# A delta-rule mixer's last turns and an expert dispatch put into one stage, with the order of each engine's queue rewritten

## The reference

```python
h = h + _L0_attn_ref(_layernorm(h))      # gated delta rule, 16 heads of 64
h = h + _L0_ffn_ref(_layernorm(h))       # 32 experts, 4 per token, 256 places each
...
# mixer, per head: S = S * exp(g); S = S + k (beta * (v - S k)); o = S q
# then o * silu(z), RMS norm, W_out
# experts:
probs = softmax(x @ gate_w.T); topk_w, topk_idx = top_k(probs, 4); topk_w /= topk_w.sum(-1)
pos = place of the row among the rows of its expert, in token order
buf = zeros((E, C + 1, h)).at[e_s, slot].set(x[t_s])          # the dispatch
expert_out = silu_and_mul(buf @ w_gate_up) @ w_down
routed = scatter-add of expert_out * topk_w (0 where pos >= 256)
shared = silu_and_mul(x @ shared_w_gate_up) @ shared_w_down
return routed + shared
```

## Time and profile before

| | us |
|---|---|
| median of 3 runs (lowest, highest) | 2871.31 (2869.2, 2872.5) |
| profiled execution, first to last instruction | 2864.9 |
| PE busy in it | 2380.9 (83%) |
| DVE busy | 2012.3 (70%) |
| ACT busy | 1292.8 (45%) |
| POOL busy | 851.1 (30%) |
| mean granted TensorE clock, share of full speed | 0.908 |

### The profile page before, as it was taken

How to read it: one execution, slowest core, us unless ns; L and a number is a source line. 1 busy time by engine, 2 the same in 40 slices (tenths; PEclk the granted TensorE clock), 3 DMA queues, 4 the chain that set the end, 5 groups by cost and what they waited for, 6 DMA issues and landing times. The chain is left out here.

```text
span 2864.9 us, 53688 instructions
## 1 busy us (share of the span) xinstructions
PE 2380.9 (83%) x19286; PEld 1823.1 (64%) x19286; DVE 2012.3 (70%) x4812; ACT 1292.8 (45%) x3118; POOL 851.1 (30%) x708
## 2 busy tenths in 40 slices
PE   7999998996468989898989898777552948899798
PEld 6777777885446777676767677555431845577454
DVE  4888884334468888888888888952663447896673
ACT  1444442111457777676767777743000314444132
POOL 2111100001023333333333333331577037650110
PEclk9999998996679999999999999988665978899799
DMA  4210001003102222222222222221211952210000
GB/s 152 88 59 29 13 7 56 22 25 121 64 20 49 53 52 53 54 53 54 53 54 53 53 53 52 49 68 35 88 37 19 295 174 74 57 47 1 24 22 27
DMA packets 274342, 168.97 MB, mean 59 GB/s; under 512 B 182847, under 2 KB 250318, under 8 KB 273728
## 3 DMA queue, kind: packets, MB, share of 16 engines
q1 hardware_dynamic: 247949, 140.28, 17.3%
q0 software_dynamic: 26112, 25.03, 3.3%
HBM read 99.23 MB, written 73.45 MB: 60 GB/s over the span
## 5 line engine op out<-in xcount | busy, mean ns | idle before, releaser
L1333 POOL TENSOR_TENSOR qd<-decay,qm 114x456 f32<-114x456 f32 x128 | 163.7, 1299 | 551.0 <-DVE qm L1448 467.0
L1838 PEld LDWEIGHTS d_ps<-d_xT,resid 128*128 128x128 f32 x1024 | 197.1, 194 | 46.1 <-issue 29.0
L1838 PE MATMUL d_ps<-d_xT,resid 128*128 128x228 f32 x1024 | 215.7, 363 | 12.3 <-DMA d_xT<-normed_t 12.3
L1429 DVE TENSOR_TENSOR ue<-ue,elim_tmp 128x30 f32<-128x30 f32 (+14 forms) x480 | 211.9, 441 | 16.8
L2578 POOL DMA_INDIRECT s_eo<-rows_y,slots_all x128 | 154.3, 1206 | 146.5 <-POOLq L2390 108.5
L1491 DVE SCALAR_TENSOR_TENSOR y_v<-raw,taps,y_v 128x228 f32<-128x228 f32 x384 | 164.4, 500 | 47.4 <-ACT y_v L1643 47.4
L1427 DVE TENSOR_TENSOR elim_tmp<-ue 128x30 f32<-128x30 f32 (+14 forms) x480 | 179.1, 373 | 25.2 <-issue 9.8
L1605 ACT ACTIVATE decay<-d_ps,gates 114x114 f32<-114x114 f32 x512 | 138.0, 362 | 85.0 <-DVE nt L1461 50.9
L1491 DVE SCALAR_TENSOR_TENSOR y_qk<-raw,taps,y_qk 128x228 f32<-128x228 f32 x384 | 145.0, 452 | 23.6 <-ACT y_qk L1643 23.6
L2142 POOL DMA_INDIRECT rows_x<-r_xn,slot x128 | 144.1, 1126 | 52.4 <-issue 50.6
L1616 ACT ACTIVATE gl<-upto,gates 114x114 f32<-114x114 f32 x512 | 156.1, 393 | 0.4
(11 more groups left out here) (343 smaller groups left out, 5559.7 us busy)
## 6 DMA issues: line engine op xcount, KB each, us to landing
rows_x<-zero_row SPq DMA_DIRECT2D x4, 2048.0 KB
ue<-blocks_n SPq DMA_DIRECT2D x16, 512.0 KB, 5.0
blocks_u<-ue SPq DMA_DIRECT2D x16, 512.0 KB, 2.8
blocks_v<-on SPq DMA_DIRECT2D x16, 512.0 KB, 2.9
e_x<-rows_x SPq DMA_DIRECT2D x32, 256.0 KB, 4.5
e_gu<-L_ffn_w_gate_up SPq DMA_DIRECT2D x32, 256.0 KB, 4.4
rows_y<-e_y SPq DMA_DIRECT2D x32, 256.0 KB, 3.4
blocks_n<-nt SPq DMA_DIRECT2D x96, 64.0 KB
```

Of the source, the lines that this page charges most:

```text
L1333: pool.tensor_tensor(qd[p.par][s][:, hs(u), :].rearrange("p (a o b) t -> p a o b t", o=2, b=2)[:, :, o], e[o][:, :, :].rearrange("p (a b) ...
L1429: step = dve.tensor_tensor(ue[:, 0:j, j + 1:], ue[:, 0:j, j + 1:], part, ALU.subtract)
L1838: last = pe.matmul(ps[:, f % 2, (t % 2) * W:(t % 2 + 1) * W], w_qkv[:, k, t * 128:(t + 1) * 128], xT[:, k, :], start=(k == 0), stop=(k == ...
```

## The change

`route` goes; its work is done in `delta_net`, in turns 15 to 17, which each engine now runs from its own `last_turns` with the order written out by hand. Turn 14 and all before it stay.

- *Rows in slots from 0 on.* `c.resid` is used from slot 0; the output weights move from slots 24 to 31 to 26 to 33. SP loads groups 0 to 3 when the last projection is done, 4 and 5 when the last gate product is, 6 when the output products of pair 13 are, 7 at the very end; for groups 6 and 7 (slots 24 to 31) the first two of eight pieces of the output weights are kept a second time (`w_late`, in `d_xT`'s place).
- *Dispatch from turn 15.* `scatter(0)` begins in the turn that makes the last decay weights; the normalised and turned rows lie in tiles that the mixer no longer uses (`raw`, `y_qk`, `y_v`, `nt`, `qd`, `ue`), the slots in four new ones.
- *Solves in halves.* Pairs 14 and 15 (`Pair.last`) are solved sample after sample, two chains at a time, in banks 0, 1, 6 and 7 (`vbank`, `xbank`); banks 2 to 5 go to the routing.
- *Other engines.* For these pairs DVE scales the gates (pair 14 and 15) and clears the update tiles, which POOL did.
- *Shared expert last.* All `gate_up` and `down` come after the last solve.

The diff, cut to its core. In it each call stands on a line of its own; here several share one. SP:

```diff
+                def load_rows(g):
+                    if g >= GROUPS - 2:
+                        for s in range(2):
+                            sp.wait_ge(h_out[s], 16 * (2 * g + 2))
+                    sp.dma_start(c.resid[:, g * GS:(g + 1) * GS, :],
+                                 hid[g * GS:(g + 1) * GS].rearrange("b s d -> s b d")).then_inc(hid_in[g], 16)
+                def last_turns():
+                    iteration(Pair(0, 14))
+                    sp.wait_ge(qkv_mm, PAIRS * 8)
+                    for g in range(EARLY):
+                        load_rows(g)
+                    sp.dma_start(w_late[:, :, :], dr["L0_attn_W_out_t"].rearrange("(k p) n -> p k n", p=128)[:, 0:2, :]).then_inc(late_in, 16)
+                    iteration(Pair(0, 15), proj=False)
...
+                    sp.wait_ge(wo_mm, 2 * PAIRS - 4)
+                    load_rows(6)
+                    iteration(Pair(0, 16), a=False, proj=False, rows=(4, 5))
+                    iteration(Pair(0, 17), a=False, proj=False, z=False)
+                    sp.wait_ge(wo_mm, 2 * PAIRS)
+                    load_rows(7)
```

POOL, from the end of turn 15's own work on (`done` is pair 14, later pair 15):

```diff
+                def scatter(g, s):
+                    pool.wait_ge(slot_r, g + 1)
+                    for k in range(TOPK):
+                        pool.indirect_dma_start(
+                            out=rows_x, out_offset=bass.IndirectOffsetOnAxis(ap=slot[g % XN][:, s, k:k + 1], axis=0),
+                            in_=rxn_t[g][:, s, :], in_offset=None, bounds_check=SLOTS - 1, oob_is_err=False).then_inc(scat[g % XN], 16)
...
+                    power(1); scatter(0, 0); power(2); scatter(0, 1); scatter(0, 2); scatter(0, 3)
+                    mask_blocks(p); done = Pair(0, 14); scatter(1, 0); scatter(1, 1)
+                    gate_power(done, 0); gate_power(done, 1); power(3); scatter(1, 2); scatter(1, 3)
+                    for s in range(GS):
+                        scatter(2, s)
+                    scatter(3, 0); power(4); scatter(3, 1); power(5); scatter(3, 2); scatter(3, 3)
+                    done = Pair(0, 15); scatter(4, 0); scatter(4, 1); scatter(4, 2); scatter(4, 3); power(6)
+                    scatter(5, 0); gate_power(done, 0); gate_power(done, 1)
+                    scatter(5, 1); scatter(5, 2); scatter(5, 3); scatter(6, 0)
+                    power(7); scatter(6, 1); scatter(6, 2); scatter(6, 3)
+                    for s in range(GS):
+                        scatter(7, s)
```

DVE, from `weights(p, 3)` of turn 15 on (`p` is pair 15, `r` pair 14, then pair 15):

```diff
+                    statistics(0); residual(done, 0); eliminate(r, 24, 29); normalise(0)
+                    weights(p, 4); query_mask(p, 2); weights(p, 5); eliminate(r, 29, 31); turn_inverse(r)
+                    gate_silu(r, 1); query_mask(p, 3); residual(done, 1); weights(p, 6); weights(p, 7)
+                    gate_silu(r, 2); gate_silu(r, 3); statistics(1); choose(0); clear_corner(r, 0); normalise(1)
+                    place(0); statistics(2); choose(1); share(0); gated(r, 0); gated(r, 1); clear_corner(r, 1)
+                    clear_rows(Pair(0, 15), 0); place(1); share(1); normalise(2); gated(r, 2); gated(r, 3); ch.end()
+                    r, done = Pair(0, 15), Pair(0, 14)
+                    gate_mean(done, 0); gate_mean(done, 1); clear_rows(r, 1); eliminate(r, 1, 5); choose(2)
+                    statistics(3); place(2); scale_rows(done, 0); scale_rows(done, 1); gate_silu(r, 0); gate_silu(r, 1)
+                    normalise(3); share(2); residual(done, 0); eliminate(r, 5, 14); gate_silu(r, 2); gate_silu(r, 3)
+                    choose(3); residual(done, 1); eliminate(r, 14, 18); place(3); eliminate(r, 18, 26)
+                    statistics(4); eliminate(r, 26, 31); turn_inverse(r); normalise(4); share(3); statistics(5)
+                    choose(4); place(4); clear_corner(r, 0); normalise(5); share(4); statistics(6); choose(5)
+                    gated(r, 0); gated(r, 1); clear_corner(r, 1); place(5); share(5); gated(r, 2); gated(r, 3)
+                    done = Pair(0, 15)
+                    gate_mean(done, 0); gate_mean(done, 1); normalise(6); scale_rows(done, 0); scale_rows(done, 1)
+                    shared(0); choose(6); residual(done, 0); residual(done, 1); place(6); share(6); shared(1)
+                    add_shared(0); statistics(7); shared(2); add_shared(1); normalise(7); shared(3); add_shared(2)
+                    choose(7); shared(4); add_shared(3); place(7); share(7)
...
```

PE, from the last output product of turn 15 on; pair 15 is solved like pair 14, with groups 4 and 5 between:

```diff
+                    output_product(done, 1); turn(0); gate_logits(0)
+                    value(r, 0, True); value(r, 1, True); join(r, 0, True); join(r, 1, True); counts(0)
+                    inverse(r, 0); inverse(r, 1); turn(1); substitute(r, 0, 0); substitute(r, 0, 1); gate_logits(1)
+                    carry(r, 0); carry(r, 1); substitute(r, 1, 0); substitute(r, 1, 1); counts(1)
+                    outputs(r, 0); outputs(r, 1); join(r, 2, True); join(r, 3, True); value(r, 2, True); value(r, 3, True)
...
+                    turn(4); value(r, 0, False); gate_logits(4); value(r, 1, False); counts(4); join(r, 0, False); join(r, 1, False)
...
+                    done = Pair(0, 15)
+                    gate_up(0); turn(6); output_turn(done, 0); gate_logits(6); output_product(done, 0); gate_up(1)
+                    output_turn(done, 1); counts(6); output_product(done, 1); down(0); gate_up(2); down(1); turn(7)
+                    gate_up(3); down(2); gate_logits(7); gate_up(4); down(3); counts(7); gate_up(5); down(4)
+                    for g in range(5, GROUPS):
+                        if g + 1 < GROUPS:
+                            gate_up(g + 1)
+                        down(g)
```

More of the change, by code:

```diff
@@ L1125, in need, with group_stats, group_scale, group_norm @@
         eng.wait_ge(sem, count)
[L1128 to L1149, removed]
+def group_stats(dve, ch, slots, stats, mv, rstd, var_ready):
+    for s in range(GS):
+        ch.note(dve.bn_stats(stats[:, s, :], slots[:, s, :]))
+    ch.sync()
+    for s in range(GS):
+        ch.note(dve.bn_aggr(mv[:, s, :], stats[:, s, :]))
+    ch.sync()
+    dve.tensor_scalar(rstd[:, :], mv[:, :, 1], LN_EPS, None, ALU.add).then_inc(var_ready, 1)
+def group_scale(dve, ch, slots, mv, rstd, xn, rstd_ready, n):
+    dve.wait_ge(rstd_ready, n)
+    for s in range(GS):
+        last = dve.tensor_scalar(xn[:, s, :], slots[:, s, :], mv[:, s, 0:1], rstd[:, s:s + 1], ALU.subtract, ALU.mult)
+        if s < GS - 1:
+            ch.note(last)
+    ch.sync()
+    return last
+def group_norm(dve, ch, slots, stats, mv, rstd, xn, var_ready, rstd_ready, n):
+    group_stats(dve, ch, slots, stats, mv, rstd, var_ready)
+    return group_scale(dve, ch, slots, mv, rstd, xn, rstd_ready, n)
+EARLY = 4
+def delta_net(c, hid, xts, slots_all, gates_all, rows_x):
     nc, dr = c.nc, c.dram
@@ L1204, in hs, with vbank, xbank, strand @@
+        scat = [c.gpsimd_dma_sem(f"scattered{p}") for p in range(XN)]
+        hid_in = [c.sem(f"r_hid_in{g}") for g in range(GROUPS)]
+        def vbank(r, m):
+            return m % 2 if r.last else (4, 5, 0, 1)[m]
+        def xbank(r, m):
+            return 6 + m % 2 if r.last else (6, 7, 2, 3)[m]
+        def strand(r, q, m):
+            return 4 * (m // 2) + 2 * q + m % 2 if r.last else 4 * q + m
         def hs(g):
@@ L1259, in iteration @@
                         store_h(p.shift(-2), 0)
+                    if rows:
+                        sp.wait_ge(z_mm, 4 * PAIRS)
+                        for g in rows:
+                            load_rows(g)
                     if z:
@@ L1317, in _ @@
                         iteration(Pair(j, 4 + k))
[L1318 to L1321, removed]
+                last_turns()
+                sp.wait_ge(hid_in[GROUPS - 1], 16)
             @block.gpsimd
@@ L1903, in join @@
                         pe.wait_ge(qm_r, r.n * 4 + 8)
+                    if r.last and s:
+                        pe.wait_ge(xc_r, r.n * 8 + strand(r, 1, g) + 1)
                     pe.sem_inc(pe_gate, 1)
@@ L2365, in experts @@
+                first_turns(iteration)
+                with pe.Fori(0, LOOPS) as j:
+                    for k in range(2):
+                        iteration(Pair(j, 4 + k))
+                last_turns()
 def experts(c, rows_x, rows_y):
@@ L3340, in program @@
         c.resid = c.arena[0:S, :, :]
-        c.stage(delta_net, hid, xts)
-        routed(c, rows_x, hid)
+        mixed(c, rows_x, hid, xts)
         c.stage(factorised_mlp, out)
```

932 lines of the change are left out of this document (643 added, 289 removed).

## The result

| | before | after |
|---|---|---|
| median, us (lowest to highest of 4 runs) | 2871.15 (2869.2 to 2872.5) | 2789.53 (2786.97 to 2792.49) |
| ratio, 95% interval | | 0.9713 (0.9694 to 0.9733) |
| profiled execution: time, span, us | span 2864.9 | 2791.91, 2790.2 |

The account below looks back on a forecast made before the run. The dispatch was taken as bound by POOL's own queue. Span 2864.9 less 81 us (earlier experts' start) plus 3 (semaphore clearing) gave 2786.5; with 6.4 kept outside the span, 2793 us, range 2770 to 2822.

Parts of the forecast that it names:

- What bounds it: Old dispatch stage: bound by POOL's own queue, 128 scatters at one per 1.42 us; other engines' work hides under it.
- part 1: Turn 15, routing of group 0: choice can begin at 1899, first scatter at 1910.7, 116 us earlier.
- Part 2: POOL's own work from the first scatter on: 202.6 us together, so at best POOL ends at 2113.
- Part 3: Pair 14 solved in halves: joins from 1900.2, halves end at 1921.2 and 1936.8, turn 15 ends 21 us later.
- Part 4: Turn 16: DVE's and POOL's queues meet at group 4's power, near 1995; pair 15's last product at 2045.
- Part 5: Tail after 2045: PE's shared-expert products precede group 7's counts; slot 7 at 2110, experts at 2139, 81 us earlier.
- rival (b): PE's tail runs at the high clock, slot 7 at 2089 no longer stops POOL: 2777 us; chance 0.08.
- Part 6: Side costs: early loads covered; SP's clearing of 91 semaphores in the experts takes 5.2 us, priced at 3.
- (a): POOL's scatters slow down beside a full DVE: 10 to 36 us more, 2803 to 2829; at its worst 0.05.
- (c): Solves of pairs 14 and 15: halves don't cover each other, each pair costs 54 us, not 37: 2821; chance 0.06.
- (e): Scatters start early but POOL's fixed order holds them at a mixer wait; waits of 21 us doubled, 2814; chance 0.03.
- (d): POOL's scatters hold DVE's two-input operations in elimination and routing, making it slower than before: 2930 us; chance 0.03.

Follow-up runs that it names:

- e3b: Changed kernel plus four idle powers on POOL behind scatter 0, ahead of the masks of pair 15: median 2803.45 us, ratio 0.9763.
- e4: Changed kernel with POOL's power of group 4 moved ahead of the four scatters before it: median 2787.64 us, ratio 0.9715.
- e8: Changed kernel with pair 15's first joins ahead of group 4's counts on PE and the corner cleared before group 4's places on DVE: 2781.38 us, ratio 0.9681.
- e1: Changed kernel with group 7's normalisation, logits, counts and places ahead of the shared expert's work of groups 2 to 4: 2778.14 us, ratio 0.9677.
- e2: Changed kernel with the shared expert left out altogether (output lacks that term): median 2781.71 us, ratio 0.9689.
- e5: Changed kernel plus 42 unused products on PE between the counts of group 3 and the turn of group 4: median 2801.60 us, ratio 0.9755.

## Why the prediction was right, step by step

- *What bounds it, and part 1:* right. First scatter 1910.07 (forecast 1910.7), choice of group 0 at 1898.89 (1899).
- *Part 2:* right. From the first scatter's start to the last one's end POOL takes 222.8 us, 18.2 of them in waits: 204.6 of its own, against 202.6. Scaling on DVE takes 1.23 us, clearing 0.91.
- *Part 3:* right within 5 us. The joins of pair 14 start at 1900.2 as forecast; its halves end at 1919.2 and 1932.3, forecast 1921.2 and 1936.8.
- *Part 4:* the meeting of the queues was right (`power(4)` at 1996.21, forecast 1995.3; DVE waited 2.21 us for it), and e3b and e4 show that each slip counts. Mis-sized was the solve of pair 15: last product over at 2049.8, not 2045. Its joins start at 2010.3, not 2008, and from there it takes 39.5 us; I had taken the 37 us that I had forecast for pair 14, and pair 14 itself took 32.1. The first half is what is long, 25.0 us against 19.0: `outputs` took 6.43 us at the low clock instead of 3.32, and PE waited 1.98 us for the corner. The order in front of it, joins behind `counts(4)` and the corner behind `place(4)`, is worth 5.9 us (e8).
- *Part 5:* the times came out (slot 6 at 2075.9 for 2075, `power(7)` 2082.25 for 2082, slot 7 at 2109.5 for 2110, experts 2138.87 for 2139), **for a wrong reason**. The step that failed is the one that took the clock of the scatter stage, 0.65, for the tail and so made PE's sum the limit. The clock was 0.91 [window 2049.80:2109.50], and three of the five `gate_up` up to `counts(7)` took 3.2 to 3.3 us (the others 5.7 and 4.8). At a high clock I had slot 7 at 2089 and called that rival (b), though my own sum had `power(7)` at 2082. Its condition came true and its time did not: the reload of the last rows lets nothing of group 7 start before 2080, and from `power(7)` (2082.25) to scatter 7 it takes 17.0 us even in e1, which gives 2099. The other 11 us are the shared expert's work standing between its steps, which e1 took out. I had priced the order as a sum of PE's products; it is a chain through three engines. That the times came out is luck: the solve ended 4.8 us late, and the tail from there to slot 7 took 59.7 us where I had 65.
- *Part 6:* the gap on SP is there, 5.6 us for 5.2:

```profile
2148.73 0.38 SPq L2807 DMA_DIRECT2D e_gu<-L_ffn_w_gate_up  x1
2154.68 0.24 SPq L2823 DMA_DIRECT2D rows_y<-e_zero  x1
```

  The first row is the last load ahead of the clearing, the second the store behind it. The cost is 0.5 us, not 3, as the loads already issued covered it. And I took 6.4 us for what lies outside the span, by setting one execution's span against another's median; the runs that list both have 1.7 to 3.0. Both errors, some 7 us too much, were made up for by the 6.5 us that the profiled execution of before had been short of its second profile behind the experts' start.
- *Rivals:* (a) is small, 2.4 us in all: the scatters' mean is 1145 ns, (73.3 + 36.3 + 37.0) / 128 from the groups' busy times, against 1126. (c) did not come: pair 14's halves took 19 and 13 us from the first joins on. (e) did not come. (d) is refuted where it had to show, in the elimination of pair 15, all of it beside scatters:

```profile
L1583 DVE TENSOR_TENSOR elim_tmp<-ue x30: 121/349/431, 1937.5 to 1993.7; 128x30 f32<-128x30 f32 x2, 128x58 f32<-128x58 f32 x2, 128x84 f32<-128x84 f32 x2, 128x108 f32<-128x108 f32 x2
L1585 DVE TENSOR_TENSOR ue<-ue,elim_tmp x30: 191/349/432, 1937.7 to 1993.9; 128x30 f32<-128x30 f32 x2, 128x58 f32<-128x58 f32 x2, 128x84 f32<-128x84 f32 x2, 128x108 f32<-128x108 f32 x2
```

  None of the 60 is held: the longest takes 0.43 us.

## What to carry to other kernels

When work is put among the instructions of a queue that others wait on, price the place and not the amount: 11.5 us on POOL cost 11.2 ahead of the masks and nothing ahead of the first scatter, where POOL waits anyway, and 5.8 us cost 0.4 behind `power(5)`, ahead of a wait of 6.65. In the tail of a stage follow the last group's steps from engine to engine and put what belongs to other groups behind them; the sum of one engine's products said little here. And judge a forecast by its steps: here the experts' start came within 1 us while the step that gave it was wrong.

## What the runs showed of the hardware

- DVE's two-input operations were held beside POOL's multiplications, and not beside its powers or its indirect DMAs. One elimination operation of pair 14 in the changed kernel, beside POOL's gate scaling that started at 1874.38 and took 1.90 us:

```profile
1874.49 1.98 DVE L1583 TENSOR_TENSOR elim_tmp<-ue 128x168 f32<-128x168 f32 x1
1876.51 0.33 DVE L1585 TENSOR_TENSOR ue<-ue,elim_tmp 128x168 f32<-128x168 f32 x1
```

  1.98 us against 0.33 for its twin. The Trainium skill, SBUF — State Buffer, section "Who interferes with whom", has this: a DVE instruction with two SBUF inputs contends with a GpSimd instruction that reads SBUF, and the ports that the two share are an exclusive lock. The trace agrees for POOL's multiplication. Beside the scatters no hold is seen: the 60 elimination operations of pair 15 took at most 0.43 us. Nor is one seen beside POOL's power of 114x16 from 1855.22 to 1858.20: the seven elimination operations that start in that time took 0.38 to 0.40 us each, and one of the same length (128x228) took 0.40 beside the scatters too. In the kernel before, the elimination of pair 15 had such holds too (its longest operation took 1.98 us).
- PE, idle for 23.75 us before `turn(4)`, was granted 0.50, the 1.2 GHz level, in that gap and in the 20 us after it (to 2019.2), and the logits took nearly twice their time (3.30 against 1.78). From 2024.0 to 2029.0 it was granted 0.97, and in `outputs` behind that 0.50 again (2029.0 to 2035.3). In e2, with less work on PE, the tail had 0.62 in the mean. In e5 PE was busy for 37 us at 0.97, and 26 us after that `outputs` ran at 0.50 again (2037.2 to 2043.7); no run here shows why.
- The clearing of 91 semaphores on SP takes 5.6 us.
